# Keys and values of two groups in one 512-wide product, and a shorter routing step, in a fused cross-attention and mixture-of-experts block

## What is computed

```python
# x: (64, 64, 256), ctx: (64, 64, 256); kv input is ctx and normed x, 128 positions a sequence
def attention(draft, ctx, ...):
    q = rms_norm((draft @ Wq.T).reshape(b, 64, 16, 128), q_norm_w)
    kv_in = concatenate([ctx, draft], axis=1)
    k = rms_norm((kv_in @ Wk.T).reshape(b, 128, 4, 128), k_norm_w)
    v = (kv_in @ Wv.T).reshape(b, 128, 4, 128)
    q, k = rope(q, pos_q), rope(k, pos_kv)
    probs = softmax(q @ k.T / sqrt(128))        # each group of k, v serves 4 heads
    return (probs @ v) @ Wo.T
def ffn(y, ...):
    top_v, top_i = top_k(softmax(y @ w_router), 2)
    top_v = top_v / sum(top_v)
    routed = sum of top_v[e] * (silu(y @ w_gate[e]) * (y @ w_up[e])) @ w_down[e] * 2.5
    shared = (silu(y @ ws_gate) * (y @ ws_up)) @ ws_down
    return routed + shared
x = x + tanh(g_xattn) * attention(layernorm(x), ctx, ...)
x = x + tanh(g_ffn) * ffn(layernorm(x), ...)
```

## Time and profile before

| | us |
|---|---|
| median of 3 runs | 1221.59 (1221.35 to 1222.02) |
| the profiled execution | 1223.99 |
| its span | 1222.2 |
| TensorE busy in the span | 1199.6 (98%) |
| VectorE, GpSimd, ScalarE busy | 1037.9, 941.1, 903.5 |

### The profile page before, as it was taken

How to read it: one execution, slowest core, us unless ns; L and a number is a source line. 1 busy time by engine, 2 the same in 40 slices (tenths; PEclk the granted TensorE clock), 3 DMA queues, 4 the chain that set the end, 5 groups by cost and what they waited for, 6 DMA issues and landing times.

```text
span 1222.2 us, 31455 instructions
## 1 busy us (share of the span) xinstructions
PE 1199.6 (98%) x8765; PEld 1113.0 (91%) x8766; DVE 1037.9 (85%) x3014; ACT 903.5 (74%) x3774; POOL 941.1 (77%) x1124
## 2 busy tenths in 40 slices
PE   6899999999999999999999999999999999999999
PEld 3788999999999999999999999999999999999887
DVE  8788999999999999999989999988888777777554
ACT  7978787887888778887888877877777646666422
POOL 2778888888888888888888888888888525555585
PEclk9999999999999999999999999999999999999999
DMA  6634233332222222223333333332235636555485
GB/s 178 201 105 127 83 99 104 111 97 90 90 90 90 90 92 93 90 95 94 96 96 114 107 101 99 105 102 80 75 108 151 225 105 192 158 164 159 149 274 183
DMA packets 141079, 148.55 MB, mean 122 GB/s; under 512 B 13824, under 2 KB 124672, under 8 KB 140256
## 3 DMA queue, kind: packets, MB, share of 16 engines
q1 hardware_dynamic: 126096, 125.97, 34.2%
q0 software_dynamic: 6480, 17.77, 4.0%
q10 hardware_dynamic: 8448, 4.20, 1.2%
HBM read 66.93 MB, written 80.76 MB: 121 GB/s over the span
## 4 chain that ended last, share of the span: by engine, by line
PE 92%; DVE 4%; ACT 3%; issue 1%; DMA 0%; SPq 0%; DVEq 0%; ACTq 0%
PE b_kv L1801 14%; PE b_q L1787 14%; PE b_o L1885 13%; PE b_sc L1859 9%; PE b_aT L1874 9%; PE b_pT L1867 5%; PE b_qT L1848 4%; PE b_q L2121 3%; PE b_kv L2121 3%; PE b_kT L1844 2%; PE b_kT L2181 1%; PE b_o L2181 1%; PE b_kv L2181 1%; PE b_q L2181 1%; PE b_aT L2138 1%; PE b_pT L2138 1%
## 5 line engine op out<-in xcount | busy, mean ns | idle before, releaser
L1801 PE MATMUL b_kv<-w_group,kv_in_hi 128*128 128x256 f32 x992 | 204.9, 304 | 0.0
L979 ACT ACTIVATE probs<-b_sc,neg_max 128x128 f32<-128x128 f32 x512 | 180.6, 371 | 2.6 <-DVE neg_max L1343 2.1
L773 POOL TENSOR_TENSOR q_rot<-q_rot,q_sin 128x512 f32<-128x512 f32 x128 | 176.7, 1381 | 7.2 <-DVE q_sin L1333 2.4
L769 POOL TENSOR_TENSOR qk_r<-qk_me,minus_half 128x6 f32<-128x6 f32 x128 | 172.0, 1344 | 10.1
L1801 PEld LDWEIGHTS b_kv<-w_group,kv_in_hi 128*128 128x128 f32 x992 | 161.3, 190 | 7.3 <-issue 0.4
L1787 PE MATMUL b_q<-w_group,kv_in_hi 128*128 128x512 f32 x496 | 164.8, 413 | 0.4 <-DVE q_sin L1333 0.4
L1885 PE MATMUL b_o<-wo_hi,aT_hi 128*128 128x256 f32 x480 | 143.5, 299 | 0.3 <-DVE aT_lo L1357 0.3
L1859 PE MATMUL b_sc<-kT,qT 128*128 128x128 f32 x1024 | 136.3, 276 | 6.2 <-ACT qT L968 4.5
L776 POOL TENSOR_TENSOR q_rot<-q_rot,qk_r 128x512 f32<-128x512 f32 x128 | 133.7, 1044 | 10.0
L1801 PE MATMUL b_kv<-w_group,kv_in_lo 128*128 128x256 f32 x496 | 139.6, 282 | 0.0
L962 ACT ACTIVATE junk<-b_q 128x128 bf16<-128x128 f32 x512 | 134.0, 283 | 0.0
(11 more groups left out here) (332 smaller groups left out, 3977.3 us busy)
## 6 DMA issues: line engine op xcount, KB each, us to landing
xs_scratch<-zeros SPq DMA_DIRECT2D x34, 1032.0 KB, 6.2
s_in<-xs_scratch SPq DMA_DIRECT2D x71, 129.0 KB
yT_scratch<-yT SPq DMA_DIRECT2D x32, 256.0 KB
routed<-ys_scratch SPq DMA_DIRECT2D x32, 256.0 KB, 4.3
w_hi_all<-w_scratch SPq DMA_DIRECT2D x3, 1536.0 KB, 14.4
x_in<-in_x SPq DMA_DIRECT2D x32, 128.0 KB, 2.3
ctx_raw<-in_ctxT SPq DMA_DIRECT2D x32, 128.0 KB, 2.5
trig_scratch<-sincos SPq DMA_DIRECT2D x8, 512.0 KB, 5.9
```

The source lines that it names most:

```text
L769: nc.gpsimd.tensor_tensor(qk_r[g % 2][:], qk_me[:], minus_half[:, 0:REP + NB], ALU.pow).then_inc(r_ready, 1)
L773: nc.gpsimd.tensor_tensor(q_rot[g % 2][:], q_rot[g % 2][:], q_sin[g % 2][:], ALU.add) \
L979: last = nc.scalar.activation(probs[:, j, :], b_sc[:, j * P:(j + 1) * P], ACT.Exp, bias=neg_max[g % 2][:, j:j + 1], accum_out=row_sum[g % ...
L1801: last = nc.tensor.matmul(b_kv[:, s * 2 * HD:(s + 1) * 2 * HD], kv_in[p][a][:, c, 2 * s:2 * s + 2, :], wkv_of(b, c)[:, g % KVH, :], start= ...
```

## The change

- `b_kv` becomes three banks. The keys and values of two groups (g and g+1) for one sequence fill one bank in six products 512 wide (`keys_values_of_two`), whose moving operand is two stretches of 256 columns, one of each group's weights. Sequence 0 of the next two groups is done at the end of each odd unit, from unit 5, sequence 1 at the end of each even unit, from unit 6. Units 2 to 5 still do single groups (`keys_values`), so unit 5 does both, and unit 125 does none.
- To free two banks, transposed queries and transposed probabilities share `b_qp`, and transposed keys share `b_sc` with the scores. So `heads_T` waits for the exponentials of the unit before. The transposed inputs and the ranks go to `b_aT`, the logits to `b_qp`. So `attend` waits for the reader of what lies in `b_aT` (`rk_read`, `x_lo`, `yT_lo` in g = 0, 1, 2), waits that stood at the start of the next unit; and `router` waits for `probs_out`.
- VectorE: `read_ranks`, `normed_lo` and `tokens_lo` move ahead of `turn_keys`. Per tile there are five routing operations less: the two halves of the share and its product with the gate become one; one comparison gives both picks; the sum of `seen` goes to GpSimd (in the loop), and the row's start is a third small product in `ranks` (`starts`) in place of a multiply-add. Four tiny operations in unit 5 and one in unit 4 prepare constants.
- ScalarE: `lead_tanh` moves from the end of the unit with g = 3 into the next unit, behind `key_squares` and ahead of `queries_out`.

The diff, cut to its core (`...` where lines are left out):

```diff
-        b_q, b_kv, b_qT, b_kT, b_sc, b_pT, b_aT, b_o = [
-            bank(n) for n in ("b_q", "b_kv", "b_qT", "b_kT", "b_sc", "b_pT", "b_aT", "b_o")]
-        b_count = b_table = b_kT
-        b_angle = (b_sc, b_pT, b_aT)
-        b_sg, b_shT, b_sT, b_sy = [b_q, b_kv], [b_qT, b_sc], [b_kT, b_o], [b_aT, b_pT]
-        b_early = (b_q, b_kv, b_pT, b_aT), (b_qT, b_sc, b_pT, b_aT)
-        b_gate, b_up, b_down = (b_q, b_kv), (b_kT, b_o), (b_sc, b_qT, b_aT, b_pT)
+        b_q = bank("b_q")
+        b_kv = ctx.enter_context(nc.psum_tensor("b_kv", [P, 3 * 512], F32))
+        b_qp, b_sc, b_aT, b_o = [bank(n) for n in ("b_qp", "b_sc", "b_aT", "b_o")]
+        b_kv0, b_kv1, b_kv2 = [b_kv[:, 512 * n:512 * (n + 1)] for n in range(3)]
+        b_count = b_table = b_qp
+        b_angle = (b_sc, b_qp, b_o)
+        b_sg, b_shT, b_sT, b_sy = [b_q, b_kv0], [b_kv1, b_sc], [b_qp, b_o], [b_aT, b_kv2]
+        b_early = (b_q, b_kv0, b_kv2, b_aT), (b_kv1, b_sc, b_kv2, b_aT)
+        b_gate, b_up, b_down = (b_q, b_kv0), (b_qp, b_o), (b_sc, b_kv1, b_aT, b_kv2)
+
+        def kv_bank(g, s):
+
+            return 1 if s == 1 else 2 * (g % KVH // 2)
+
+        def kv_of(g):
+
+            both = b_kv[:].rearrange("p (k j w n) -> p k j w n", k=3, j=2, w=2)[:, :, g % 2, :, :]
+            return both[:, 0:2, :, :] if g % KVH < 2 else both[:, 2:0:-1, :, :]
...
+                    if g == 0 and not first:
+                        need(pool, rk_done, t - 1)
+                        nc.gpsimd.tensor_tensor(seen[:], seen[:], mask[:], ALU.add).then_inc(seen_ready, 1)
...
+                if g % 2 == 1:
+                    need(act, k_turned, 2 * n)
...
+                    if g == 0 and not first:
+                        lead_tanh(t - 2)
                     if not (first and u == 0):
...
-                    if g == 3 and not (end or first and p == 0):
-                        lead_tanh(t - 1)
...
-                nc.vector.tensor_copy(top_f[:], top_i[:, 0:TOPK])
+                nc.vector.tensor_copy(top_f[:], top_i[:, 0:TOPK]).then_inc(pick_ready, 1)
+                need(dve, pick_ready, 2 * t + 1)
+                each = [P, TOPK, E]
+                nc.vector.tensor_tensor(pick[:], expert_no[:].unsqueeze(1).to_broadcast(each),
+                                        top_f[:].unsqueeze(2).to_broadcast(each), ALU.is_equal).then_inc(pick_ready, 1)
                 need(dve, lead_done, t + 1)
-                nc.vector.tensor_scalar(share[:, 0:1], lead_t[:], ROUTED_SCALE / 2, ROUTED_SCALE / 2, ALU.mult, ALU.add)
-                nc.vector.tensor_scalar(share[:, 1:2], lead_t[:], -ROUTED_SCALE / 2, ROUTED_SCALE / 2, ALU.mult,
-                                        ALU.add).then_inc(share_ready, 1)
-                need(dve, share_ready, t + 1)
-                for n in range(TOPK):
-                    last = nc.vector.tensor_scalar(pick[:, n, :], expert_no[:], top_f[:, n:n + 1], None, ALU.is_equal)
-                last.then_inc(pick_ready, 1)
-                nc.vector.tensor_scalar(y_share[p], share[:], gates[:, 1:2], None, ALU.mult)
-                need(dve, pick_ready, t + 1)
+                need(dve, wsin_ready, 8)
+                nc.vector.scalar_tensor_tensor(out=y_share[p], in0=gate_signed[:], scalar=lead_t[:], in1=gate_half[:],
+                                               op0=ALU.mult, op1=ALU.add)
+                need(dve, pick_ready, 2 * t + 2)
+                need(dve, seen_ready, t + 1)
                 nc.vector.tensor_tensor(mask[:], pick[:, 0, :], pick[:, 1, :], ALU.add).then_inc(mask_ready, 1)
 
             def rows_of_tokens(t, p):
 
                 need(dve, rk_read, t + 1)
-                nc.vector.tensor_reduce(rank[:], ranked[:], AX.X, ALU.add).then_inc(rank_step, 1)
-                need(dve, rank_step, 2 * t + 1)
-                nc.vector.scalar_tensor_tensor(out=row_f[:], in0=top_f[:], scalar=float(STRIDE), in1=rank[:], op0=ALU.mult,
-                                               op1=ALU.add).then_inc(rank_step, 1)
-                need(dve, rank_step, 2 * t + 2)
+                nc.vector.tensor_reduce(row_f[:], ranked[:], AX.X, ALU.add).then_inc(rank_step, 1)
+                need(dve, rank_step, t + 1)
                 nc.vector.tensor_copy(row_i[p][:], row_f[:]).then_inc(row_ready, 1)
 
-            def read_ranks(t):
+            def read_ranks(t, bank):
                 need(dve, rk_done, t + 1)
-                nc.vector.tensor_tensor(ranked[:], pick[:], b_kT[:, D:D + E].unsqueeze(1).to_broadcast([P, TOPK, E]),
+                nc.vector.tensor_tensor(ranked[:], pick[:], bank[:, D:D + E].unsqueeze(1).to_broadcast([P, TOPK, E]),
                                         ALU.mult).then_inc(rk_read, 1)
-                nc.vector.tensor_tensor(seen[:], seen[:], mask[:], ALU.add) \
-                  .then_inc(seen_ready, 1)
+                if isinstance(t, int) and t >= TILES - 2:
+                    nc.vector.tensor_tensor(seen[:], seen[:], mask[:], ALU.add).then_inc(seen_ready, 1)
...
+                        nc.vector.tensor_scalar(starts[:], expert_no[:], float(STRIDE // P), None, ALU.mult)
...
+                            for to, m, sign in ((gate_signed, 0, 1), (gate_signed, 1, -1), (gate_half, 0, 1), (gate_half, 1, 1)):
+                                nc.vector.tensor_scalar(to[:, m:m + 1], gates[:, 1:2], sign * ROUTED_SCALE / 2, None,
+                                                        ALU.mult).then_inc(wsin_ready, 1)
...
                     score_max(n, g)
+                    if g == 0 and not first:
+                        read_ranks(t - 2, b_aT)
+                    if g == 1 and not end:
+                        normed_lo(t + 1, 1 - p)
+                    if g == 2 and not (first and p == 0):
+                        tokens_lo(t - 1, 1 - p)
...
+            def keys_values_of_two(n, g, s, t, p):
+
+                if s == 0:
+                    need(pe, k_turned, 2 * (n - 2))
+                    if g == 0:
+                        need(pe, ctx_lo, t)
+                        need(pe, x_lo, t)
+                else:
+                    need(pe, k_turned, 2 * n - 1)
+                o = 512 * kv_bank(g, s)
+                for c in range(DC):
+                    for a, b in PASSES:
+                        last = nc.tensor.matmul(b_kv[:, o:o + 512].rearrange("p (g n) -> p g n", g=2),
+                                                kv_in[p][a][:, c, 2 * s:2 * s + 2, :],
+                                                wkv_of(b, c)[:, g:g + 2, :],
+                                                start=(c == 0 and (a, b) == PASSES[0]),
+                                                stop=(c == DC - 1 and (a, b) == PASSES[-1]))
+                if s == 1:
+                    last.then_inc(kv_done, 2)
 
...
             def heads_T(n, g):
+                need(pe, exp_done, n)
                 need(pe, k_ready, n + 1)
                 for s in range(NB):
-                    last = nc.tensor.transpose(b_kT[:, s * P:(s + 1) * P], k_rot[g % 2][:, s, :], ident[:])
+                    last = nc.tensor.transpose(b_sc[:, s * P:(s + 1) * P], k_rot[g % 2][:, s, :], ident[:])
                 last.then_inc(kT_done, 1)
                 need(pe, q_ready, n + 1)
                 for h in range(REP):
-                    last = nc.tensor.transpose(b_qT[:, h * P:(h + 1) * P], q_rot[g % 2][:, h, :], ident[:])
+                    last = nc.tensor.transpose(b_qp[:, h * P:(h + 1) * P], q_rot[g % 2][:, h, :], ident[:])
...
-                    if g == 2 and not end:
-                        need(pe, x_lo, t + 1)
-                    if g == 3 and not (first and p == 0):
-                        need(pe, yT_lo, t)
                     if g == 0 and not first:
                         need(pe, lg_copied, t - 1)
-                    if g == 1 and not first:
-                        need(pe, rk_read, t - 1)
...
                     if g == 3 and not (first and p == 0):
+                        need(pe, pT_out, n)
                         router(t - 1)
...
+                    if g == 0 and not first:
+                        need(pe, rk_read, t - 1)
+                    if g == 1 and not end:
+                        need(pe, x_lo, t + 1)
+                    if g == 2 and not (first and p == 0):
+                        need(pe, yT_lo, t)
                     if not (first and u < 1):
                         attend(n - 1, g - 1)
                     if first and 2 <= u < 6:
                         pe.wait_ge(w_lo, 2 * (u - 2) + 2)
                     if first and u < 2:
                         first_keys_values(u + 2)
-                    elif not (end and g >= 2):
+                    elif first and u < 6:
                         keys_values(n + 2, g + 2, t2, p2)
+                    elif g % 2 == 0 and not (end and g == 2):
+                        keys_values_of_two(n + 2, (g + 2) % KVH, 1, t2, p2)
+                    if g % 2 == 1 and not (first and u < 5 or end):
```

(4 more changed lines are left out.)

95 lines of the change are left out of this document (46 added, 49 removed).

## The result

The changed kernel takes **1231.15 us** (median, 1230.67 to 1232.91) against 1221.80 of the kernel before on the same chip (1221.35 to 1222.05): a ratio of **1.0078, 95% interval 1.0067 to 1.0090**. It is 0.8% slower. The forecast was 1216.7 with a range to 1222.5, so the time lies 8.7 us outside it, on the other side. The profiled execution has a span of 1231.1 us against 1222.2.

What follows compares the result with a forecast made beforehand. TensorE's list was taken to bound the attention loop. The terms -5.7 + 1.9 + 0.8 - 2.3 - 0.4 + 0.9 gave -4.8 us (-4.9 unrounded), so 1221.6 - 4.9 = 1216.7 us, range 1214.0 to 1222.5.

Steps and rivals of the forecast that it cites:

- What bounds the kernel: Attention loop: TensorE, busy 58.10 of 58.10 us a turn, sets the time; other engines have slack on the mean.
- Moved and new waits: Loop units: `attend`, `heads_T`, later `turn_keys` and key sum, and `seen` on GpSimd all called hidden, at no cost.
- Rival 3: Units with g = 1: key sum slips over 0.7 us, TensorE stands before the key transposes; 1226 us, chance 0.08.
- Wider products, -5.7: Units 6 to 124: six 512 wide products replace twelve 256 wide, 0.048 us less per unit, -5.7 us.
- The rival of two stretches: Wide products: two stretches cost like two products (0.238 us), so nothing is saved; 1222.4 us, chance 0.15.
- The Trainium skill's figure for the gap of a single product: Wide products: a small fixed gap, 2.5 ns, saves 15 ns a unit, 1.8 us in all; 1220.6 us, chance 0.10.
- Unit 5, +1.9 with the end: Unit 5 does both product kinds, +1.4, and waits for turned keys, +0.7; units 125 and 126 give -0.2.
- Third `ranks`, +0.8: TensorE's third small product in `ranks`: 0.03 us, 30 times in the loop, +0.8 us.
- Tanh, -2.3 and -0.4: ScalarE's later tanh removes the excess of 13 units with u = 0, -2.3 us, and -0.4 in unit 12.
- the fewer operations on VectorE: Five routing operations less, about 0.5 us a tile freed on VectorE, counted as none in the loop.
- `seen` on GpSimd, 0: `seen` on GpSimd, some 0.2 us ahead of the cosine table and next unit's scales, called hidden in the slack.
- Router in unit 127, +0.9: Unit 127: `router` waits for the copy of probabilities, shared products stand behind the wait; +0.9 us, once.

Runs made afterwards that it cites:

- b_lo_first: Kernel before with one step alone: VectorE's `normed_lo` ahead of `layer_stats2` and `turn_keys` in units with g = 1; 1.0093.
- a_narrow: Changed kernel with each 512 wide product of keys and values made as two 256 wide ones, same place and banks; 1.0093 of the kernel before.
- a_best: Changed kernel with `sin_table` ahead of the scatter except in the last pair, SyncE's weight load held back, unit 5's two-group product first; 0.9969 of the kernel before.
- b_tanh: Kernel before with ScalarE's `lead_tanh` alone moved one unit later, behind the key squares of the unit with g = 0; 1.0001.
- the kernel of three edits: The same kernel as a_best: changed kernel with `sin_table` earlier, weight load held back, unit 5's products reordered; 0.9969 of the kernel before.
- a_best_ops: The kernel of three edits with five unused 128 x 1 VectorE operations put back in the routing part of units with g = 0; 1.0002 of the kernel before.
- the second trace: The changed kernel run once more, nothing edited; 1.0085 of the kernel before.
- a_no_hold: Changed kernel with `sin_table` earlier, unit 5's products reordered and GpSimd's `layer_rstd` ahead of `cos_table`, the weight load not held back; 1.0063 of the kernel before.

## Why the prediction was wrong, point by point

**What bounds the kernel: right for TensorE, incomplete.** TensorE's list did set the turn. But VectorE's and GpSimd's slack was judged by the mean of a turn and by TensorE's next need. Neither shows the meeting of `sin_w` and the piece.

**The step that failed** is in *Moved and new waits*: "`turn_keys` falls 0.34 us later in g = 1, and GpSimd's key sum with it [...] still 0.7 ahead of 548.21: hidden." The 0.34 was right (0.31 measured), and TensorE had the key sum in time. What was left out is the rest of GpSimd's list, which rival 3 calls nearly without idle time: 0.31 there is 0.48 to 0.50 at `sin_w`, and `sin_w` holds a VectorE operation that had no room. In the changed kernel 22 units of the loop carry +7.9 us where -1.1 was forecast; alone in the kernel before the step costs 11.5 (`b_lo_first`). That is 9.0 of the 13.8 us between the forecast and the measured difference of the spans (-4.9, +8.9). Rival 3 had the origin and the sign and 0.08 of the chance; its place (TensorE before the key transposes, units with g = 1) and its threshold (0.7 us) were wrong.

**Wider products, -5.7:** the row was read nearly right, 0.040 a unit and not 0.048, where nothing waits. In the kernel as it stands the width gives some 2 us (`a_narrow`, read from the loop). The rival of two stretches is refuted. The Trainium skill's figure for the gap of a single product ("TensorE: Matmul & The Clock Gate", Back-to-back issue gap) would by the prediction's estimate have the unit 0.015 shorter; the trace says 0.040.

**Unit 5, +1.9 with the end:** right at the front, +2.08 for +2.1, and 0.67 of it comes back by the order of the two products (`a_best`), close to the 0.7 that the text gives to the wait for turned keys. Units 125 and 126 together gave +0.1 for -0.2.

**Third `ranks`, +0.8:** L2069 and L2070 start 0.026 us apart in the changed kernel, in 32 tiles (26 of them in the loop, not the 30 that the text has): the term stands.

**Tanh, -2.3 and -0.4:** the place was right, -2.19 with the tanh alone (`b_tanh`); unit 12 gave -0.20 there and -0.49 in the changed kernel. But alone it gives nothing in all. The stall moved to u = 1 where VectorE is late next; it pays only beside the fewer operations on VectorE, which the sum had **at 0** with "costs and gains nothing there". Five operations of that size are worth 2.1 us in the kernel of three edits (`a_best_ops`). The two terms came out right in sum, which was luck, and wrong each.

**`seen` on GpSimd, 0:** a loss of 1.2 us in the changed kernel's loop, 3.6 in the kernel before.

**Router in unit 127, +0.9:** the wait is there. The router starts 1.29 us behind the transposes of the probabilities (975.07 to 976.36), where it started 0.44 behind them (964.84 to 965.28): +0.85. Whether the end is longer by it is not settled, since ends differ by more than that between traces.

**What was missing altogether:** the scatter that lands late in unit 123, +2.3, since it went out 0.28 us ahead of SyncE's stores and no longer 1.28. The chance meeting at the start, +1.0, and the end, -1.2 here and +1.8 in the second trace, could not be forecast.

## What to carry to other kernels

The slack of an operation is the smallest over all that stand behind it in its own engine's list, not the slack to the engine you think of as the bound: follow a shift of 0.3 us down the list until it is absorbed by a wait. Two engines that hold each other up, as VectorE and GpSimd do here, can turn that shift into the full length of the other's operation, so look at what will run beside what after the shift, not only at what waits for what. And when you take a stall away, ask first who has been catching up during it.

## What the runs showed of the chip

A VectorE operation with both inputs in SBUF stood still while a GpSimd tensor operation ran: 608 columns in 0.76 us alone, 0.87 us with 0.23 of overlap, 1.51 and 2.00 us with `sin_w` ending later; 384 columns of `probs` in 0.60 and in 1.44 us. A cast of two columns, with one input, took 0.17 and 0.54. Which of the two stands goes by the starts for `probs` and `cos_w`: in all traces here `cos_w` grows from 1.02 to 1.31 us or more, and `probs` goes on, where `cos_w` starts 0.02 us or more behind it, and `probs` stands for the whole of `cos_w` where that starts first. It does not go by the recorded starts for the piece and `sin_w`: in the changed kernel the piece starts 0.31 us first, in the last 0.28 us of the scatter, and yet it stands while `sin_w` takes its 1.02 us. Why is open. `aT_lo`, whose one input comes from the matrix banks, took 0.68 or 0.69 us in every row shown. The scatter's own time on GpSimd did not hold VectorE, though it took 1.43 us in place of 1.19 beside the piece. The Trainium skill has this rule ("SBUF — State Buffer", Who interferes with whom): an operation of VectorE with two SBUF inputs and a GpSimd operation that reads SBUF exclude each other for a whole instruction, by order of issue. The traces agree that one stands for the whole of the other in the rows with two inputs in SBUF, and with the order for `probs`, not for the piece. The cast has one input, and that sentence does not cover it.

I had not expected that a margin of 0.02 us on who starts first would be worth 0.46 us a unit, nor that it would fall differently in two traces of one program (unit 121 of the changed kernel, 7.70 and 7.21 us). A scatter of 128 rows landed within 6.7 us of its start before, when the first of 2 MB of zeros went out 1.28 us after it. It took 9.6 us when they went out 0.28 us after it and a load of 1.5 MB 1.54 after it, and 7.9 us with that load held back; without the hold it took 7.5 in `a_no_hold`. What sets the rest was not separated.
